# Expert stage of a four-layer megakernel: fourth buffers for split weights and rows, and the weight split moved ahead of the gate

## The chip, the cores and the metric

The kernel runs on one core of a Trainium2 chip. A core has five engines that run their own instruction streams in order and meet only at semaphores: TensorE (PE in the rows, its weight loads PEld), VectorE (DVE), ScalarE (ACT), GpSimd (POOL) and SyncE (SP), which here only starts DMA transfers. The metric is the device time of one execution in microseconds (us).

## The reference, cut to what matters

The program is a stack of four layers on x of 8 x 128 tokens by 256 features. Each layer is a normalised cross attention and then a feed-forward part with a mixture of experts. The change touches only the routed experts of the second layer:

```python
T = 1024 tokens, K = 4, E = 32 experts, C = 2*T*K//E = 256 rows each, H = 256, I = 128
buf = zeros((E, C, H)).at[sorted_eid, pos].set(x[tok], mode='drop')   # rows gathered by expert
gu = einsum('ech,ehf->ecf', buf, w13);  g, u = split(gu, 2, axis=-1)
act = silu(g) * u
eo = einsum('eci,eih->ech', act, w2)
out_slots = eo[sorted_eid, pos]                                       # and back to the tokens
```

## The kernel before, in words

Everything is written by hand: each engine's stream is a Python function, all orders are those of the code, and semaphores carry the dependencies. Before the expert stage the normalised rows of all tokens are scattered in DRAM to the `seats` of their experts. Then 32 experts pass through one software pipeline, one expert per turn of the loop.

For expert k the work is this. SP loads 384 KB of float32 weights (`expert_weights`, L549) and 288 KB of rows (`expert_rows`, L556: 256 rows of 256 features and 32 numbers of destination). PE turns the rows with four float32 transposes (`expert_turn`, L1520). ACT and DVE split the turned rows in a high and a low float16 part (`expert_x`: ACT L1062 twice, DVE L2451 twice, then DVE L2454 for the destinations). The weights are split in the same way (`expert_split`: ACT L1054 high, then DVE L2460 low). PE does gate and up with 12 matmuls (L1535). ACT takes silu of the gate (L1070), DVE multiplies it by up (`expert_gated`, L2470), ACT and DVE split the product (`expert_h`: L1078, L2476), PE does the down product with 6 matmuls (L1550), ACT copies it out (`expert_out`, L1086), and POOL scatters it in two indirect transfers (L749) to `slots` in DRAM.

The orders of one turn k of the loop are:
- PE: turn k+1, gate and up k, down k-1.
- ACT: rows' high part k+1, silu k, weights' high part k+2, product's high part k, copy out k-1.
- DVE: rows' low parts and destinations k+1, product k, weights' low part k+2, product's low part k.
- SP: weights k+3, rows k+2, and the last output row of expert k-2 (L562), which waits until expert k-2 has been copied out (`e_y`). So each transfer behind it starts only after that copy.

There are four buffers of raw weights (`e_w`), but three of split weights (`e_split`) and three of rows (`e_x`). The split of expert k+2 therefore waits for the down product of expert k-1 (`e_down`), and the rows of k+2 wait until those of k-1 are turned and their destinations read. After the last expert SP waits for all scatters and loads the `slots` back.

Of the kernel before, what the change touches and what calls it, by code (L numbers as in the profile page):

```python
# [26 lines left out]
F16 = mybir.dt.float16  # L27
# [4 lines left out]
ACT = mybir.ActivationFunctionType  # L32
AX = mybir.AxisListType

P = 128
B, S, D = 8, 128, 256
# [9 lines left out]
E0, F0, FS0 = 8, 176, 352  # L46
SHARED0 = -(-FS0 // P)
E1, F1 = 32, 128
# [29 lines left out]
def build(nc, a, out):  # L78

    with ExitStack() as ctx:  # L80
# [23 lines left out]
        ident = sb("ident", [P, P])  # L104
# [51 lines left out]
        class Arena:  # L156
# [4 lines left out]
            def take(self, shape, dt=F32, rows=P):  # L161
# [27 lines left out]
        ar = Arena()  # L189
# [21 lines left out]
        ar = Arena()  # L211
        f_s = ar.take([2, HALF])
        f_g = ar.take([2, HALF])
        f_h = ar.take([2, HALF])
# [4 lines left out]
        f_wT = ar.take([T], rows=E0)  # L219
        f_cmp = ar.take([B, E0, E0])  # L220
        f_eq = ar.take([B, E0, E0])
        f_rk = ar.take([B, E0])
# [18 lines left out]
        m_place = ar.take([B, E1])  # L241
        m_w = ar.take([B, TOP1])
        m_dest = ar.take([E1, CT]).bitcast(U32)
        e_x = ar.take([3, CT, ROW])
        wq_f = arena[:, ar.at:ar.at + T].rearrange("p (w o d) -> p w o d", w=2, o=KD)
        wq_diag = arena[:, ar.at:ar.at + HALF].rearrange("p (k o) -> p k o", k=4)
        e_xT = ar.take([2, 2, KD, CAPACITY], F16)
# [6 lines left out]
        last_rows = k3_raw[0:E1, :]  # L254
        e_w = [W[:, 1, :], wb[:, :, :].rearrange("p a b -> p (a b)")[:, 0:WROW],
               wb[:, :, :].rearrange("p a b -> p (a b)")[:, WROW:2 * WROW], W[:, 0, :]]
        e_split = [W16[:, 1, :, :], e_w16, W16[:, 0, :, :]]
        x_rms = xn


# [175 lines left out]
        def _(sp):  # L436
# [114 lines left out]
            def expert_rows(k):  # L551

                if k >= 3:
                    sp.wait_ge(sem("e_turn"), k - 2)
                    sp.wait_ge(sem("e_dest"), k - 2)
                sp.dma_start(e_x[:, k % 3, :, :], seats[k * CAPACITY:(k + 1) * CAPACITY, :].rearrange("(p c) d -> p c d", c=CT))\  # L556
                    .then_inc(sem("ex_in", k % 3), 16)

            def last_row(k):

# [11 lines left out]
            def loads_1():  # L572
                for k in range(4):
                    expert_weights(k)
                sp.wait_ge(sem("seated"), 16 * B * TOP1)
                for k in range(3):
                    expert_rows(k)
                for k in range(E1):
                    if k >= 1 and k + 3 < E1:
                        expert_weights(k + 3)  # L580
                    if k >= 1 and k + 2 < E1:
                        expert_rows(k + 2)
                    if k >= 2:
# [246 lines left out]
        def _(act):  # L830
# [216 lines left out]
            def expert_split(k):  # L1047

                act.wait_ge(sem("slot_in", k % 4), 16 * (k // 4 + 1))
                if k == 2:  # L1050
                    act.wait_ge(sem("down_done"), tiles(2))
                if k >= 3:
                    act.wait_ge(sem("e_down"), k - 2)
                nc.scalar.activation(e_split[k % 3][:, 0, :], e_w[k % 4], ACT.Copy, scale=WSCALE).then_inc(sem("ew_hi"), 1)  # L1054

            def expert_x(k):

# [288 lines left out]
        def _(pe):  # L1346
# [163 lines left out]

            def expert_turn(k):

                pe.wait_ge(sem("ex_in", k % 3), 16 * (k // 3 + 1))
                if k < 2:
                    pe.wait_ge(sem("gated"), EXPERT)
                else:
                    pe.wait_ge(sem("e_xlo"), KD * (k - 1))
                for c in range(KD):
                    for r in range(CT):
                        last = nc.tensor.transpose(ps[:, k % 2, c * CAPACITY + r * P:c * CAPACITY + (r + 1) * P],  # L1520
                                                   e_x[:, k % 3, r, c * P:(c + 1) * P], ident[:, :])
                last.then_inc(sem("e_turn"), 1)

            def expert_gate_up(k):

                pe.wait_ge(sem("ew_lo"), k + 1)
                pe.wait_ge(sem("e_xlo"), KD * (k + 1))
                if k >= 2:
                    pe.wait_ge(sem("gated"), EXPERT + k - 1)
                else:  # L1530
                    pe.wait_ge(sem("wi"), 2)
                for g in range(2):
                    for c in range(KD):
                        for i, w in THREE:
                            last = nc.tensor.matmul(ps[:, 2 + k % 2, g * CAPACITY:(g + 1) * CAPACITY],  # L1535
                                                    e_split[k % 3][:, w, g * D + c * P:g * D + (c + 1) * P],
                                                    e_xT[:, k % 2, i, c, :], start=(g == 0 and c == 0 and i + w == 0),
                                                    stop=(c == KD - 1 and w == 1), skip_group_check=True)
                last.then_inc(sem("gu_done"), 1)

            def expert_down(k):

                pe.wait_ge(sem("h_lo"), EXPERT + k + 1)
                if k < 2:
                    pe.wait_ge(sem("shared_read"), 1)
                else:
                    pe.wait_ge(sem("e_y"), k - 1)
                for r in range(CT):
                    for w, i in THREE:
                        last = nc.tensor.matmul(ps[:, 4 + k % 2, r * D:(r + 1) * D], f_h16[:, k % 2, i, r * P:(r + 1) * P],  # L1550
                                                e_split[k % 3][:, w, 2 * D:3 * D], start=(r == 0 and i + w == 0),
                                                stop=(w == 1), skip_group_check=True)
                last.then_inc(sem("e_down"), 1)

# [446 lines left out]
        def _(dve):  # L2001
# [445 lines left out]
            def expert_x(k):  # L2447

                dve.wait_ge(sem("e_xhi"), KD * (k + 1))
                for c in range(KD):  # L2450
                    nc.vector.scalar_tensor_tensor(e_xT[:, k % 2, 1, c, :], ps[:, k % 2, c * CAPACITY:(c + 1) * CAPACITY],  # L2451
                                                   normw[:, c:c + 1], e_xT[:, k % 2, 0, c, :], ALU.mult, ALU.subtract)\
                        .then_inc(sem("e_xlo"), 1)
                nc.vector.tensor_scalar(m_dest[:, k, :], e_x[:, k % 3, :, D + k], -1.0, NOWHERE, ALU.mult, ALU.add)\  # L2454
                    .then_inc(sem("e_dest"), 1)

            def expert_split(k):

                dve.wait_ge(sem("ew_hi"), k + 1)
                nc.vector.scalar_tensor_tensor(e_split[k % 3][:, 1, :], e_w[k % 4], WSCALE, e_split[k % 3][:, 0, :],  # L2460
                                               ALU.mult, ALU.subtract).then_inc(sem("ew_lo"), 1)

            def expert_gated(k):
# [488 lines left out]
```

## Time and profile before

| | us |
|---|---|
| median of 3 runs | 1033.53 (1028.81 to 1034.68) |
| the profiled execution, its own time | 1037.46 |
| its span, first to last instruction | 1035.6 |
| busy in the span: PE / DVE / ACT / POOL | 859.2 / 677.9 / 521.2 / 326.0 |

The expert stage runs from about 304 to 426 us of the span. A row of a timeline names the start, the duration, the engine, the line, the operation with output and input, and in brackets how long the engine had been idle and what released it. `arena`, `W` and `wb` are on-chip memory that several names share (`e_x`, `f_h16`, `e_y` and one split buffer lie in `arena`), `ps` is PSUM, `in_w` the weights in DRAM.

### The profile page before, as it was taken

To read this page: it belongs to the slowest core of one execution; us is meant where nothing else is said; L and a number is where in the kernel's file an instruction comes from. 1 tells how busy PE (TensorE), PEld (TensorE's weight loads), DVE (VectorE), ACT (ScalarE), POOL (GpSimd) and SP (SyncE) were. 2 spreads that over 40 slices of the span, in tenths; PEclk is the share of its full clock that TensorE was granted. 3 is DMA by queue.
4 is the path that set the end of the run, shared out by engine and by line. 5 is a ranking of instruction groups with operands and counts; after the bars stand their busy time and mean duration, and the time that the engine had idled before them with its cause. 6 is when DMAs were issued, how large, how long until landed. Compare 5 with 4: busy or idle time off the path is not lost. (4 is left out here: it accounts for less than half of the span.)

```text
span 1035.6 us, 17165 instructions
## 1 busy us (share of the span) xinstructions
PE 859.2 (83%) x6369; PEld 532.9 (51%) x6369; DVE 677.9 (65%) x1402; ACT 521.2 (50%) x840; POOL 326.0 (31%) x267
## 2 busy tenths in 40 slices
PE   5978999776227776797979998778799999999997
PEld 3434665463216564574545554445455556555554
DVE  7985888787817667266336479645778657744343
ACT  4714345445117767336558743455456786533332
POOL 2531343312744555303025662100355333200000
PEclk9988999988659999897879999999999999999999
DMA  8973433310246677331013453111256445433332
GB/s 267 324 254 107 129 107 114 93 33 1 114 151 189 211 225 218 117 113 46 18 32 122 123 170 106 46 32 47 70 174 182 129 129 167 144 105 95 107 94 85
DMA packets 60191, 129.12 MB, mean 125 GB/s; under 512 B 9267, under 2 KB 25025, under 8 KB 60114
## 3 DMA queue, kind: packets, MB, share of 16 engines
q1 hardware_dynamic: 55506, 119.17, 37.4%
q0 software_dynamic: 4608, 8.94, 2.3%
q8 instruction: 47, 0.77, 0.3%
q14 instruction: 30, 0.25, 0.1%
HBM read 83.95 MB, written 48.27 MB: 128 GB/s over the span
## 5 line engine op out<-in xcount | busy, mean ns | idle before, releaser
L1448 PE MATMUL ps<-turned_buf,W 128*128 128x512 f16 x576 | 136.8, 388 | 5.7 <-DVE ctx_sb L2280 1.8
L2280 DVE SCALAR_TENSOR_TENSOR ctx_sb<-ps,ctx_sb 128x512 f32<-128x512 f32 x96 | 66.2, 690 | 111.0 <-PE ps L1448 80.7
L1448 PE MATMUL ps<-turned_buf,wb 128*128 128x512 f16 x576 | 133.5, 382 | 0.0
L2287 DVE TENSOR_TENSOR ctxT<-ctx_sb,ctxT 128x512 f16<-128x512 f32 x96 | 71.4, 744 | 70.7 <-ACT ctxT L1023 70.2
L761 POOL TENSOR_SCALAR W<-W 128x768 f32<-128x768 f32 x32 | 68.6, 2145 | 127.8 <-ACT wb L1035 64.1
L1023 ACT ACTIVATE ctxT<-ctx_sb 128x512 f16<-128x512 f32 x96 | 60.2, 627 | 94.4 <-DVE ctx_sb L2280 94.3
L1015 ACT ACTIVATE ctx_sb<-ps 128x512 f32<-128x512 f32 x96 | 57.3, 597 | 99.3 <-PE ps L1448 99.0
L1448 PEld LDWEIGHTS ps<-turned_buf,W 128*128 128x128 f16 x576 | 56.1, 100 | 69.1 <-issue 8.0
L1391 PE MATMUL ps<-turned_buf,W 128*128 128x512 f16 x360 | 87.3, 396 | 2.5 <-issue 2.5
L1448 PEld LDWEIGHTS ps<-turned_buf,wb 128*128 128x128 f16 x576 | 56.1, 99 | 59.8 <-issue 2.7
L749 POOL DMA_INDIRECT slots<-arena x64 | 62.3, 973 | 68.6 <-ACT arena L1086 56.3
L1464 PE MATMUL ps<-W,ctxT 128*128 128x256 f16 x576 | 70.8, 273 | 5.4 <-DVE x L2296 3.7
L1464 PE MATMUL ps<-wb,ctxT 128*128 128x256 f16 x576 | 72.0, 276 | 3.8 <-DVE ctxT L2287 3.2
L705 POOL TENSOR_TENSOR arena<-arena,wb 128x512 f32<-128x512 f32 x28 | 42.6, 1523 | 87.9 <-DVE arena L2221 87.9
L1464 PEld LDWEIGHTS ps<-wb,ctxT 128*128 128x128 f16 x576 | 55.6, 99 | 21.5 <-DVE ctxT L2287 4.9
L1464 PEld LDWEIGHTS ps<-W,ctxT 128*128 128x128 f16 x576 | 54.4, 98 | 23.2 <-issue 10.9
L1391 PEld LDWEIGHTS ps<-turned_buf,W 128*128 128x128 f16 x360 | 36.2, 101 | 43.4 <-issue 9.6
L1520 PE MATMUL ps<-ident,arena 128*128 128x128 f32 x128 | 22.5, 305 | 41.0 <-DMA arena<-seats 36.8
L678 POOL TENSOR_TENSOR rstd<-veps,mhalf 128x4 f32<-128x4 f32 x13 | 14.5, 1118 | 129.8 <-DVE veps L2019 129.8
L2296 DVE SCALAR_TENSOR_TENSOR x<-ps,arena,x 128x256 f32<-128x256 f32 x128 | 52.9, 475 | 2.4 <-PE ps L1464 2.4
L1403 PE MATMUL ps<-W,arena 128*128 128x256 f16 x360 | 45.5, 279 | 9.6 <-DVE arena L2228 9.6
L988 ACT ACTIVATE arena<-arena 128x512 f16<-128x512 f32 x30 | 18.7, 629 | 56.7 <-POOL arena L705 56.5
(411 smaller groups left out, 1719.4 us busy)
## 6 DMA issues: line engine op xcount, KB each, us to landing
W<-in_w SPq DMA_DIRECT2D x77, 384.0 KB, 3.6
seats<-k_st SPq DMA_DIRECT2D x8, 1152.0 KB, 10.9
arena<-seats SPq DMA_DIRECT2D x32, 288.0 KB
kept<-W SPq DMA_DIRECT2D x24, 384.0 KB, 4.0
kept<-wb SPq DMA_DIRECT2D x24, 384.0 KB, 4.2
W<-kept SPq DMA_DIRECT2D x24, 384.0 KB
wb<-kept SPq DMA_DIRECT2D x24, 384.0 KB
wb<-in_w SPq DMA_DIRECT2D x18, 384.0 KB, 11.2
```

The lines of the kernel that those rows point to most:

```text
L705: nc.gpsimd.tensor_tensor(f_h[:, half, :], f_g[:, half, :], wb[:, k % 2, half * HALF:(half + 1) * HALF], ALU.mult).then_inc(sem("h_full"), 1)
L749: nc.gpsimd.indirect_dma_start(slots, bass.IndirectOffsetOnAxis(ap=m_dest[:, k, c:c + 1], axis=0), e_y[k % 3][:, c, :], None, bounds_check ...
L761: link(nc.gpsimd.tensor_scalar(W[:, n % 2, :], W[:, n % 2, :], WSCALE, None, ALU.mult))
L1015: nc.scalar.activation(h_s[:, g % 2, :], bank(4), ACT.Silu, scale=1.0 / WSCALE).then_inc(sem("silu_done"), 1)
L1023: nc.scalar.activation(h_16[:, g % 2, 0, :], h_g[:, g % 2, :], ACT.Copy).then_inc(sem("h_hi"), 1)
L1391: last = nc.tensor.matmul(bank(2 * g + half), W16[:, k % 2, w, g * D + c * P:g * D + (c + 1) * P], x16[:, i, c, half * HALF:(half + 1) * H ...
L1403: last = nc.tensor.matmul(ps[:, 4 + t // 2, (t % 2) * D:(t % 2 + 1) * D], f_h16[:, k % 2, i, t * S:(t + 1) * S], W16[:, k % 2, w, 2 * D:3 ...
L1448: last = nc.tensor.matmul(bank(4 + n), w4[k % 4][:, w, n * D + c * P:n * D + (c + 1) * P], x16[:, i, c, half * HALF:(half + 1) * HALF], st ...
L1464: last = nc.tensor.matmul(ps[:, 6 + t // 2, (t % 2) * D:(t % 2 + 1) * D], h_16[:, g % 2, i, t * S:(t + 1) * S], w4[k % 4][:, w, 2 * D:3 * ...
L2280: nc.vector.scalar_tensor_tensor(h_g[:, g % 2, :], bank(5), 1.0 / WSCALE, h_s[:, g % 2, :], ALU.mult, ALU.mult).then_inc(sem("gated"), 1)
L2287: nc.vector.tensor_tensor(h_16[:, g % 2, 1, :], h_g[:, g % 2, :], h_16[:, g % 2, 0, :], ALU.subtract)\
L2296: ins = nc.vector.scalar_tensor_tensor(x[:, t, :], ps[:, 6 + t % 4 // 2, (t % 2) * D:(t % 2 + 1) * D], l_w[:, L - 2, t, e:e + 1], x[:, t, ...
```

## The change

Split weights and rows get a fourth buffer each. The fourth split buffer lies where `f_h` of the first layer was, the fourth buffer of rows where the first layer's router compared its scores. On ACT and on DVE the split of expert k+2 moves ahead of the silu and the product of expert k. SP issues the rows one expert further ahead (k+3 in place of k+2) and ahead of the weights.

```diff
-        e_x = ar.take([3, CT, ROW])
+        e_rows = ar.take([3, CT, ROW])
+        e_x = [e_rows[:, k, :, :] for k in range(3)] + \
+            [arena[:, f_cmp_at:f_cmp_at + CT * ROW].rearrange("p (c d) -> p c d", c=CT)]
...
-        e_split = [W16[:, 1, :, :], e_w16, W16[:, 0, :, :]]
+        e_split = [W16[:, 1, :, :], e_w16, arena[:, f_h_at:f_h_at + WROW].bitcast(F16).rearrange("p (i d) -> p i d", i=2),
+                   W16[:, 0, :, :]]
...
             def expert_rows(k):
-                if k >= 3:
-                    sp.wait_ge(sem("e_turn"), k - 2)
-                    sp.wait_ge(sem("e_dest"), k - 2)
+                if k >= 4:
+                    sp.wait_ge(sem("e_turn"), k - 3)
+                    sp.wait_ge(sem("e_dest"), k - 3)
...
-                for k in range(3):
+                for k in range(4):
                     expert_rows(k)
                 for k in range(E1):
                     if k >= 1 and k + 3 < E1:
+                        expert_rows(k + 3)
                         expert_weights(k + 3)
-                    if k >= 1 and k + 2 < E1:
-                        expert_rows(k + 2)
...
             def expert_split(k):          # ACT
                 act.wait_ge(sem("slot_in", k % 4), 16 * (k // 4 + 1))
-                if k == 2:
+                if k == 3:
                     act.wait_ge(sem("down_done"), tiles(2))
-                if k >= 3:
-                    act.wait_ge(sem("e_down"), k - 2)
+                if k >= 4:
+                    act.wait_ge(sem("e_down"), k - 3)
...
                 for k in range(E1):       # ACT
                     if k + 1 < E1:
                         expert_x(k + 1)
-                    expert_silu(k)
                     if k + 2 < E1:
                         expert_split(k + 2)
+                    expert_silu(k)
                     expert_h(k)
...
             for k in range(E1):           # DVE
                 if k + 1 < E1:
                     expert_x(k + 1)
-                expert_gated(k)
                 if k + 2 < E1:
                     expert_split(k + 2)
+                expert_gated(k)
                 expert_h(k)
```

The order of instructions on ACT in a turn in the middle of the stage, before. L1062 is the rows' high part, L1070 silu, L1054 the weights' high part, L1078 the product's high part, L1086 the copy out:

```order
L1062 ACTIVATE arena<-ps,normw 128x256 x2
L1070 ACTIVATE arena<-ps 128x256
L1054 ACTIVATE arena<-W 128x768
L1078 ACTIVATE arena<-arena 128x256
L1086 ACTIVATE arena<-ps 128x512
```

And in the changed kernel, where the same lines stand five lines later (L1067, L1059, L1075, L1083, L1091):

```order
L1067 ACTIVATE arena<-ps,normw 128x256 x2
L1059 ACTIVATE arena<-wb 128x768
L1075 ACTIVATE arena<-ps 128x256
L1083 ACTIVATE arena<-arena 128x256
L1091 ACTIVATE arena<-ps 128x512
```

The weights' part has moved from between silu and the product's part to ahead of silu.

The order on DVE in the same place, before. L2451 is the rows' low part, L2454 the destinations, L2470 the product of silu and up, L2460 the weights' low part, L2476 the product's low part:

```order
L2451 SCALAR_TENSOR_TENSOR arena<-ps,normw,arena 128x256 x2
L2454 TENSOR_SCALAR arena<-arena 128x2
L2470 SCALAR_TENSOR_TENSOR arena<-ps,arena 128x256
L2460 SCALAR_TENSOR_TENSOR arena<-W,arena 128x768
L2476 TENSOR_TENSOR arena<-arena 128x256
```

And in the changed kernel (L2456, L2459, L2465, L2475, L2481):

```order
L2456 SCALAR_TENSOR_TENSOR arena<-ps,normw,arena 128x256 x2
L2459 TENSOR_SCALAR arena<-arena 128x2
L2465 SCALAR_TENSOR_TENSOR W<-W 128x768
L2475 SCALAR_TENSOR_TENSOR arena<-ps,arena 128x256
L2481 TENSOR_TENSOR arena<-arena 128x256
```

The product, for which ACT's L1083 waits, now stands behind the weights' low part.

## Rows read from the trace of the kernel before

**Rows 1.** The expert stage: length, busy us of PE, PEld, DVE, ACT, POOL, granted clock, DMA share, GB/s

```profile
304.00:420.00 116.00, 88.58 (x675) 67.65 (x676) 79.13 (x183) 82.31 (x184) 54.50 (x56) 0.94 0.66 205
```

**Rows 2.** The transposes of rows (L1520): count, then what ended the idle time before

```profile
L1520 PE MATMUL ps<-ident,arena x128: 272/273/476, 303.9 to 417.8; 128*128 128x128 f32 x128
...
  DMA arena<-seats: 80.3, 32
```

**Rows 3.** Timeline of ACT, one undisturbed turn of the loop

```profile
313.12 0.84 ACT L1054 ACTIVATE W<-W 128x768 f16<-128x768 f32 x1 [0.64 <-PE ps L1550]
313.88 0.40 ACT L1078 ACTIVATE arena<-arena 128x256 f16<-128x256 f32 x1
314.18 0.58 ACT L1086 ACTIVATE arena<-ps 128x512 f32<-128x512 f32 x1
314.66 0.83 ACT L1062 ACTIVATE arena<-ps,normw 128x256 f16<-128x256 f32 x2
315.37 0.39 ACT L1070 ACTIVATE arena<-ps 128x256 f32<-128x256 f32 x1
316.27 0.84 ACT L1054 ACTIVATE arena<-W 128x768 f16<-128x768 f32 x1 [0.51 <-PE ps L1550]
317.02 0.40 ACT L1078 ACTIVATE arena<-arena 128x256 f16<-128x256 f32 x1
```

**Rows 4.** Timeline of DVE in the same turn

```profile
314.00 0.96 DVE L2460 SCALAR_TENSOR_TENSOR W<-W 128x768 f16<-128x768 f32 x1 [0.67 <-ACT W L1054]
314.88 0.42 DVE L2476 TENSOR_TENSOR arena<-arena 128x256 f16<-128x256 f32 x1
315.52 0.88 DVE L2451 SCALAR_TENSOR_TENSOR arena<-ps,normw,arena 128x256 f16<-128x256 f32 x2 [0.23 <-ACT arena L1062]
316.31 0.25 DVE L2454 TENSOR_SCALAR arena<-arena 128x2 uint32<-128x2 f32 x1
316.38 0.42 DVE L2470 SCALAR_TENSOR_TENSOR arena<-ps,arena 128x256 f32<-128x256 f32 x1
```

**Rows 5.** Timeline of PE in the same turns and the next

```profile
312.20 0.83 PE L1550 MATMUL ps<-W,arena 128*128 128x256 f16 x6
...
315.35 0.83 PE L1550 MATMUL ps<-arena 128*128 128x256 f16 x6 [0.57 <-DVE arena L2476]
...
318.50 0.83 PE L1550 MATMUL ps<-W,arena 128*128 128x256 f16 x6 [0.53 <-issue]
319.54 0.66 PE L1520 MATMUL ps<-ident,arena 128*128 128x128 f32 x4 [0.21 <-DMA arena<-seats]
```

**Rows 6.** Timeline of ACT, the end of the stage

```profile
418.77 0.58 ACT L1086 ACTIVATE arena<-ps 128x512 f32<-128x512 f32 x1
...
423.47 0.42 ACT L1078 ACTIVATE arena<-arena 128x256 f16<-128x256 f32 x1 [0.49 <-DVE arena L2470]
...
425.38 0.60 ACT L1086 ACTIVATE arena<-ps 128x512 f32<-128x512 f32 x1 [0.86 <-PE ps L1550]
```

**Rows 7.** Timeline of DVE, the product before that

```profile
423.01 0.42 DVE L2470 SCALAR_TENSOR_TENSOR arena<-ps,arena 128x256 f32<-128x256 f32 x1 [0.72 <-issue]
```

**Rows 8.** Timeline of SP's queue, two issues of rows

```profile
316.09 0.38 SPq L556 DMA_DIRECT2D arena<-seats  x1
...
340.04 0.38 SPq L556 DMA_DIRECT2D arena<-seats  x1
```

**Rows 9.** Timeline of PE, the transposes that used the second of them

```profile
345.99 0.66 PE L1520 MATMUL ps<-ident,arena 128*128 128x128 f32 x4 [0.94 <-DMA arena<-seats]
```

**Rows 10.** Timeline of ACT, two later turns

```profile
320.34 0.84 ACT L1054 ACTIVATE W<-wb 128x768 f16<-128x768 f32 x1 [1.31 <-PE ps L1550]
...
368.77 0.38 ACT L1070 ACTIVATE arena<-ps 128x256 f32<-128x256 f32 x1 [2.35 <-remote]
```

**Rows 11.** What SP's queue waited for in the stage: us, times, longest

```profile
SPq L562 <- ACT arena L1086: 64.7, 29, 6.5
```

**Rows 12.** Timeline of POOL, the last scatter

```profile
429.54 0.97 POOL L749 DMA_INDIRECT slots<-arena  x1 [0.30 <-issue]
```

More of the change, by code:

```diff
@@ L213, in build @@
         f_g = ar.take([2, HALF])
+        f_h_at = ar.at
         f_h = ar.take([2, HALF])
@@ L219, in build @@
         f_wT = ar.take([T], rows=E0)
+        f_cmp_at = ar.at
         f_cmp = ar.take([B, E0, E0])
@@ L243, in build @@
         m_dest = ar.take([E1, CT]).bitcast(U32)
-        e_x = ar.take([3, CT, ROW])
+        e_rows = ar.take([3, CT, ROW])
+        assert CT * ROW <= 2 * B * E0 * E0
+        e_x = [e_rows[:, k, :, :] for k in range(3)] + \
+            [arena[:, f_cmp_at:f_cmp_at + CT * ROW].rearrange("p (c d) -> p c d", c=CT)]
         wq_f = arena[:, ar.at:ar.at + T].rearrange("p (w o d) -> p w o d", w=2, o=KD)
@@ L551, in expert_rows @@
             def expert_rows(k):
-                if k >= 3:
-                    sp.wait_ge(sem("e_turn"), k - 2)
-                    sp.wait_ge(sem("e_dest"), k - 2)
-                sp.dma_start(e_x[:, k % 3, :, :], seats[k * CAPACITY:(k + 1) * CAPACITY, :].rearrange("(p c) d -> p c d", c=CT))\
-                    .then_inc(sem("ex_in", k % 3), 16)
+                if k >= 4:
+                    sp.wait_ge(sem("e_turn"), k - 3)
+                    sp.wait_ge(sem("e_dest"), k - 3)
+                sp.dma_start(e_x[k % 4], seats[k * CAPACITY:(k + 1) * CAPACITY, :].rearrange("(p c) d -> p c d", c=CT))\
+                    .then_inc(sem("ex_in", k % 4), 16)
             def last_row(k):
@@ L1049, in expert_split @@
                 act.wait_ge(sem("slot_in", k % 4), 16 * (k // 4 + 1))
-                if k == 2:
+                if k == 3:
                     act.wait_ge(sem("down_done"), tiles(2))
-                if k >= 3:
-                    act.wait_ge(sem("e_down"), k - 2)
-                nc.scalar.activation(e_split[k % 3][:, 0, :], e_w[k % 4], ACT.Copy, scale=WSCALE).then_inc(sem("ew_hi"), 1)
+                if k >= 4:
+                    act.wait_ge(sem("e_down"), k - 3)
+                nc.scalar.activation(e_split[k % 4][:, 0, :], e_w[k % 4], ACT.Copy, scale=WSCALE).then_inc(sem("ew_hi"), 1)
             def expert_x(k):
@@ L1511, in expert_turn @@
             def expert_turn(k):
-                pe.wait_ge(sem("ex_in", k % 3), 16 * (k // 3 + 1))
+                pe.wait_ge(sem("ex_in", k % 4), 16 * (k // 4 + 1))
                 if k < 2:
@@ L1520, in expert_turn @@
                         last = nc.tensor.transpose(ps[:, k % 2, c * CAPACITY + r * P:c * CAPACITY + (r + 1) * P],
-                                                   e_x[:, k % 3, r, c * P:(c + 1) * P], ident[:, :])
+                                                   e_x[k % 4][:, r, c * P:(c + 1) * P], ident[:, :])
                 last.then_inc(sem("e_turn"), 1)
@@ L1535, in expert_gate_up @@
                             last = nc.tensor.matmul(ps[:, 2 + k % 2, g * CAPACITY:(g + 1) * CAPACITY],
-                                                    e_split[k % 3][:, w, g * D + c * P:g * D + (c + 1) * P],
+                                                    e_split[k % 4][:, w, g * D + c * P:g * D + (c + 1) * P],
                                                     e_xT[:, k % 2, i, c, :], start=(g == 0 and c == 0 and i + w == 0),
@@ L1550, in expert_down @@
                         last = nc.tensor.matmul(ps[:, 4 + k % 2, r * D:(r + 1) * D], f_h16[:, k % 2, i, r * P:(r + 1) * P],
-                                                e_split[k % 3][:, w, 2 * D:3 * D], start=(r == 0 and i + w == 0),
+                                                e_split[k % 4][:, w, 2 * D:3 * D], start=(r == 0 and i + w == 0),
                                                 stop=(w == 1), skip_group_check=True)
@@ L2453, in expert_x @@
                         .then_inc(sem("e_xlo"), 1)
-                nc.vector.tensor_scalar(m_dest[:, k, :], e_x[:, k % 3, :, D + k], -1.0, NOWHERE, ALU.mult, ALU.add)\
+                nc.vector.tensor_scalar(m_dest[:, k, :], e_x[k % 4][:, :, D + k], -1.0, NOWHERE, ALU.mult, ALU.add)\
                     .then_inc(sem("e_dest"), 1)
@@ L2459, in expert_split @@
                 dve.wait_ge(sem("ew_hi"), k + 1)
-                nc.vector.scalar_tensor_tensor(e_split[k % 3][:, 1, :], e_w[k % 4], WSCALE, e_split[k % 3][:, 0, :],
+                nc.vector.scalar_tensor_tensor(e_split[k % 4][:, 1, :], e_w[k % 4], WSCALE, e_split[k % 4][:, 0, :],
                                                ALU.mult, ALU.subtract).then_inc(sem("ew_lo"), 1)
```

## The prediction

> **What bounds the kernel now.** The page comes first, for the engines' totals, then the windows of the expert stage, then the groups of waits inside it, then the timelines of ACT, DVE and PE over two turns of the loop that nothing disturbs, and last the queue of SP. The stage takes 116 us in which PE is busy 88.58, ACT 82.31 and DVE 79.13 [rows 1]. No engine is full, so a chain across engines sets the pace. Outside the stage the change moves nothing.
>
> The copy-out of expert 0 starts at 314.18 [rows 3], that of expert 28 at 418.77, with three more behind it, the last at 425.38 [rows 6]. That is 28 turns in 104.6 us, 3.74 us each.
>
> An undisturbed turn is shorter. The down product of one expert starts at 312.20 and the next at 315.35, the one after at 318.50 [rows 5]: 3.15 us, twice. The rows close the loop. The down product takes 0.83, ends at 313.03, and releases ACT's split of the weights at 313.12 [rows 3], because its buffer is the one which that product read. DVE's low part starts at 314.00, the product's low part behind it at 314.88 and takes 0.42 [rows 4], and the next down product starts at 315.35 [rows 5]. So 0.83 + 0.09 + 0.88 + 0.88 + 0.42 + 0.05 = 3.15. Three buffers of split weights make this loop.
>
> At that pace 28 turns would take 88.2 us. The other 16.4 us are lost in single turns. The waits of PE's transposes name the loads of rows every time [rows 2] (27.4 us of that total are the wait for the first rows, before the stage). Rows issued at 316.09 [rows 8] were used at 319.54 [rows 5], 3.45 us later; those issued at 340.04 [rows 8] only at 345.99 [rows 9], 5.95 us later. SP issues them late since its queue stands behind the last row of an older expert: 64.7 us of waiting for ACT's copy-out [rows 11]. A late transpose costs more than its own wait: the down product before it should have ended at 318.50 + 0.83 = 319.33, but ACT's split, which it releases, starts at 320.34 [rows 5, 10]. Once silu starts 2.35 us late though its input had been computed long before by the rows of PE [rows 10]; I count this with the 16.4 us.
>
> **The change part by part.**
>
> The fourth buffer of split weights. The split of k+2 now waits for the down product of k-2 in place of k-1. That product is a whole turn older, so the loop of 3.15 us is cut. By itself this is a gain, down to what the next chain allows.
>
> The fourth buffer of rows, and their place in SP's queue. Rows k+3 are issued where rows k+2 were. They have one turn more, at least 3.15 us, in front of the slowest transfer seen, 5.95 us. I expect the transposes' waits to go inside the stage, and with them most of the 16.4 us. The weights are issued one rows' issue later (0.38 us [rows 8]) and are split somewhat earlier in the turn. Their lead is about two turns and a half, over 8 us, so the shift is hidden. If that cover is gone it comes back as a wait of ACT, which is the third rival below.
>
> The new order. It adds no instruction, it moves two. Before, ACT's split of the weights filled the time in which DVE made the product of silu and up; the product stood ahead of the weights' low part on DVE. Now DVE does the rows' low parts and the destinations, waits for ACT's high part of the weights, does their low part, and only then the product. ACT's next instruction after silu, the product's high part, waits for all of it, and behind that instruction stand the copy-out and the rows of the next expert. So ACT and DVE go round together:
> - ACT rows' high part to DVE's rows' low part: 315.52 - 314.66 = 0.86 [rows 3, 4]
> - low parts and destinations, to DVE's next instruction: 316.38 - 315.52 = 0.86 [rows 4]
> - weights' low part, to DVE's next: 314.88 - 314.00 = 0.88 [rows 4]
> - the product: 0.42 [rows 4]
> - to ACT's waiting high part: 423.47 - (423.01 + 0.42) = 0.04 [rows 6, 7]
> - high part to copy-out: 314.18 - 313.88 = 0.30 [rows 3]
> - copy-out to the rows' high part of the next expert: 314.66 - 314.18 = 0.48 [rows 3]
>
> The sum is 3.84 us a turn. No buffer is in this loop, so no buffer can shorten it. Is PE able to follow? It was busy 88.58 us in about 31 turns, 2.85 us each, and now none of its results is needed at once: silu comes behind the split, and a product ends more than a turn before it is copied out. PE therefore runs ahead and waits. A delay of one to two us on PE is taken up by that lead, which is why I set the remaining stalls to nothing. Bounds for the turn: the same ring entered through ACT's split (0.71 from the rows to ACT's next instruction, 0.88 to DVE's low part, then 0.88 + 0.42 + 0.04 + 0.30 + 0.48 [rows 3, 4, 6, 7]) gives 3.71. That would hold if DVE's rows were never late. Above, the 16.4 us may stay in part. I take 3.84, since both of its first terms stand in every undisturbed turn.
>
> The first turns: the split of expert 2 moves into idle time, the copy-out of expert 0 gets the new order once; I put it at +0.3 us (0 to +1). In the last turns there is no split and the order is the old one. The last scatter starts at 429.54 [rows 12], behind POOL's own queue, and only shifts with the rest.
>
> **The sum.** 28 x 3.84 = 107.5 us in place of 104.6, and 0.3 at the start: +3.2 us. The profiled execution took 1037.46 us, of which 1.9 lie around its span of 1035.6. The changed kernel would take 1037.46 + 3.2 = 1040.7. The median of the runs before is 1033.5, 3.9 lower. If those runs differ outside this stage, the new median is 1036.8. If they lost 3.9 us less to late rows, which the new order swallows anyway, it is 1040.7. I take the middle, 1039.
>
> By the Trainium skill (Perfetto Trace Analysis, section Optimization Strategy) the same gap repeating on an engine can mean too little SBUF for the next tile, so too few buffers. ACT's repeated 0.51 us before the split is such a gap [rows 3], and two buffers are added here. That rule leads to the first rival.
>
> **The rivals.**
>
> Faster: the buffers decide, not the order. If the product did not have to wait for the weights' low part, for instance because the split runs so far ahead that it is over when silu ends, the turn would be 3.15 us or below, down to PE's 2.85. That gives 88.2 - 104.6 = -16.4 us, or -24.8. For it: the stalls on rows are real and the change goes for them. Against it: ACT's split comes directly behind the rows' high part of the same turn, so DVE cannot have its low part done before 0.86 + 0.86 + 0.88 us into the turn. It decides if DVE's product follows ACT's silu within 0.1 us. Time: 1033.5 - 16.4 + up to 3.9, about 1019.
>
> Slower still: the stalls stay on top of the 3.84 us. For it: one late silu had no late transfer that I can name. Against: PE's lead. With half of 16.4 left it is 1047, with all 1055.
>
> The clock: PE's granted clock is 0.94 in the stage [rows 1], nearly always the upper of its two levels (2.4 GHz). If the regular pauses of PE put it on 1.2 GHz, a turn would be 2 x 2.85 = 5.7 us, 28 of them 160 us, the whole 1088. Against: PE's share, 2.85 of 3.84, is 0.74 where it was 0.76.
>
> **How the numbers follow.** The forecast, a ring of 3.7 to 3.9 us with little left of the stalls, has 0.72, its own range is 1035 to 1044. The faster rival has 0.13, stalls on top 0.13, the clock 0.02. About 0.5%, 5.2 us, is what a measurement of this kernel tells from no change. The border at 1038.7 cuts the forecast: 0.40 of its 0.72 lie above, 0.31 within, 0.01 below. So slower is 0.40 + 0.13 + 0.02 = 0.55, same 0.31, faster 0.01 + 0.13 = 0.14. The range 1033 to 1046 leaves out the faster rival, the clock and the worse third of the stalls, 0.2 in all.
>
> **What would show it.** In the changed profile the copy-outs should follow each other every 3.8 to 3.9 us with little scatter. The wait of PE's transposes for rows should be the first one alone. ACT should wait before the product's high part in every turn, about 1 us, for DVE's product, and DVE's product should start when the weights' low part lets it, over 0.5 us after silu's end. PE should wait for DVE before gate and up or down. I am wrong if the turns are 3.2 us or shorter, or if ACT waits for transfers of weights, or if the stage keeps turns of 5 us.

## The result, and the profile after

Seven runs of each kernel on one chip: 1032.53 us median before (1028.69 to 1036.47), 1042.71 us changed (1038.09 to 1046.10). The difference of the medians is 10.2 us, the ratio 1.0107 with a 95% interval of 1.0073 to 1.0141: the changed kernel is slower. The profiled execution of the changed kernel took 1046.10 us, its span is 1044.2.

The stage in the same window as [rows 1]:

```profile
304.00:420.00 116.00, 84.32 (x666) 63.95 (x666) 77.60 (x183) 78.32 (x179) 63.82 (x56) 0.98 0.62 199
```

PE and ACT are less busy than before in the same 116 us (84.32 in place of 88.58, 78.32 in place of 82.31): fewer turns fit into them. The granted clock is 0.98 where it was 0.94; both windows hold the stage's first turns, before which PE had stood still, and from 312 on the changed kernel has 1.00.

The transposes of rows, as in [rows 2]; the second row is the idle time in front of them by releaser, with the number of waits:

```profile
L1525 PE MATMUL ps<-ident,arena x128: 272/273/477, 301.7 to 417.4; 128*128 128x128 f32 x128
...
  DMA arena<-seats: 54.9, 2
```

Two waits in place of 32, both of them the first wait before the stage (about 27.4 us, counted once for PE and once for its weight load). No transpose inside the stage waits for its rows any more. This row counts PE and PEld together. Before, the 32 were 13 waits of PE (36.8 us) and 19 of PEld (43.4 us), so PE itself waited 12 times and 9.4 us inside the stage.

One turn on ACT, to be read against [rows 3]. L1067 is the rows' high part, L1059 the weights' high part, L1075 silu, L1083 the product's high part, L1091 the copy-out:

```profile
323.50 0.58 ACT L1091 ACTIVATE arena<-ps 128x512 f32<-128x512 f32 x1
323.97 0.83 ACT L1067 ACTIVATE arena<-ps,normw 128x256 f16<-128x256 f32 x2
324.68 0.85 ACT L1059 ACTIVATE W<-W 128x768 f16<-128x768 f32 x1
325.42 0.39 ACT L1075 ACTIVATE arena<-ps 128x256 f32<-128x256 f32 x1
327.01 0.42 ACT L1083 ACTIVATE arena<-arena 128x256 f16<-128x256 f32 x1 [1.21 <-DVE arena L2475]
327.34 0.58 ACT L1091 ACTIVATE arena<-ps 128x512 f32<-128x512 f32 x1
327.81 0.83 ACT L1067 ACTIVATE arena<-ps,normw 128x256 f16<-128x256 f32 x2
```

The same turn on DVE, against [rows 4]. L2456 is the rows' low part, L2459 the destinations, L2465 the weights' low part, L2475 the product, L2481 the product's low part:

```profile
324.84 0.88 DVE L2456 SCALAR_TENSOR_TENSOR arena<-ps,normw,arena 128x256 f16<-128x256 f32 x2 [0.79 <-ACT arena L1067]
325.63 0.25 DVE L2459 TENSOR_SCALAR arena<-arena 128x2 uint32<-128x2 f32 x1
325.69 0.95 DVE L2465 SCALAR_TENSOR_TENSOR W<-W 128x768 f16<-128x768 f32 x1
326.56 0.42 DVE L2475 SCALAR_TENSOR_TENSOR arena<-ps,arena 128x256 f32<-128x256 f32 x1
327.46 0.42 DVE L2481 TENSOR_TENSOR arena<-arena 128x256 f16<-128x256 f32 x1 [0.48 <-ACT arena L1083]
```

These twelve rows hold the result. ACT's rows at 323.97, DVE's rows at 324.84, weights' low part at 325.69, product at 326.56, ending at 326.98, ACT's product high part at 327.01, copy-out at 327.34, next rows at 327.81. From 323.97 to 327.81 are 3.84 us. ACT stands still for 1.21 us in front of L1083; silu was over at 325.81, but DVE's product started only 0.75 us later, behind the weights.

PE in the same time, against [rows 5]. L1555 is down, L1525 the transposes, L1540 gate and up:

```profile
324.11 0.83 PE L1555 MATMUL ps<-W,arena 128*128 128x256 f16 x6 [0.66 <-DVE arena L2481]
324.77 0.60 PE L1525 MATMUL ps<-ident,arena 128*128 128x128 f32 x4
325.81 1.48 PE L1540 MATMUL ps<-arena 128*128 128x256 f16 x12 [0.44 <-issue]
327.94 0.83 PE L1555 MATMUL ps<-arena 128*128 128x256 f16 x6 [0.66 <-DVE arena L2481]
```

The down products start at 324.11 and 327.94, 3.83 us apart, and PE has pauses of 0.4 and 0.7 us in each turn. All waits of ACT for DVE's product in the stage:

```profile
ACT arena L1083 <- DVE arena L2475: 37.1, 32, 1.2
```

32 waits, 37.1 us. The copy-outs of experts 0, 28 and 31, as in [rows 3, 6]:

```profile
311.97 0.58 ACT L1091 ACTIVATE arena<-ps 128x512 f32<-128x512 f32 x1
```

```profile
419.60 0.58 ACT L1091 ACTIVATE arena<-ps 128x512 f32<-128x512 f32 x1
...
426.10 0.60 ACT L1091 ACTIVATE arena<-ps 128x512 f32<-128x512 f32 x1 [0.89 <-PE ps L1555]
```

From 311.97 to 419.60 are 107.6 us for 28 turns, which the prediction put at 107.5. Every one of these turns takes 3.84 to 3.89 us. ACT never waits for a transfer of weights in the stage. SP's queue still waits for ACT's copy-out (72.5 us where it was 64.7), so it is the lead of one turn more that hides the rows' transfers, not an earlier end of that wait.

### The profile page after: what moved, and what is told of

Its sections match the earlier page's. It is cut to its first block and busy times, and to the rows that moved or that the text cites. A ratio compares the mean times of both kernels' runs of the same rounds, so it can differ in the third digit from the quotient of the medians.

```text
span 1044.2 us, 17163 instructions
## 1 busy us (share of the span) xinstructions
PE 862.5 (83%) x6369; PEld 532.3 (51%) x6369; DVE 677.2 (65%) x1402; ACT 519.1 (50%) x840; POOL 335.1 (32%) x267
## 5 line engine op out<-in xcount | busy, mean ns | idle before, releaser
L1020 ACT ACTIVATE ctx_sb<-ps 128x512 f32<-128x512 f32 x96 | 57.2, 596 | 100.6 <-PE ps L1453 100.4
L754 POOL DMA_INDIRECT slots<-arena x64 | 71.6, 1119 | 62.3 <-ACT arena L1091 51.5
L1469 PE MATMUL ps<-W,ctxT 128*128 128x256 f16 x576 | 73.0, 278 | 5.4 <-DVE x L2301 3.7
L2456 DVE SCALAR_TENSOR_TENSOR arena<-ps,normw,arena 128x256 f16<-128x256 f32 x64 | 28.0, 480 | 46.1 <-ACT arena L1067 46.1
```

The lines of the kernel that those rows point to most:

```text
L754: nc.gpsimd.indirect_dma_start(slots, bass.IndirectOffsetOnAxis(ap=m_dest[:, k, c:c + 1], axis=0), e_y[k % 3][:, c, :], None, bounds_check ...
L1020: nc.scalar.activation(h_s[:, g % 2, :], bank(4), ACT.Silu, scale=1.0 / WSCALE).then_inc(sem("silu_done"), 1)
L1469: last = nc.tensor.matmul(ps[:, 6 + t // 2, (t % 2) * D:(t % 2 + 1) * D], h_16[:, g % 2, i, t * S:(t + 1) * S], w4[k % 4][:, w, 2 * D:3 * ...
```

## The experiments

All times of 28 turns are those from the copy-out of expert 0 to that of expert 28. Ratios are to the kernel before, timed beside it on the same chip, with a 95% interval. The experiments ran on different chips, so times of two kernels are compared directly only where both stood beside the kernel before on one of them.

| kernel | 28 turns, us | undisturbed turn | ratio of the time to before |
|---|---|---|---|
| before, four profiles | 104.6, 100.4, 96.3, 95.5 | 3.15 | |
| changed, two profiles | 107.6, 107.7 | 3.84 | 1.0107 [1.0073, 1.0141], 1.0139 [1.0097, 1.0182] |
| order only | 114.3 | 4.06 | 1.0086 [1.0048, 1.0124] |
| changed, DVE's order undone | 95.7 | 3.13 | 0.9853 [0.9793, 0.9913] |
| changed, both orders undone, two profiles | 90.8, 83.7 | 2.97 | 0.9851 [0.9796, 0.9906], 0.9873 [0.9811, 0.9934] |
| changed, copy-out ahead | 93.4 | 3.36 | 0.9982 [0.9942, 1.0023] |
| rows only | 88.5 | 3.15 | 0.9901 [0.9874, 0.9928] |
| split buffers only | 92.9 | 2.97 | 0.9963 [0.9931, 0.9995] |
| both orders undone, copy-out ahead | 74.2 | mostly 2.5 to 2.67 (mean of all: 2.65) | 0.9831 [0.9790, 0.9872] |

### The order undone on both engines

```diff
                     if k + 1 < E1:            # ACT
                         expert_x(k + 1)
+                    expert_silu(k)
                     if k + 2 < E1:
                         expert_split(k + 2)
-                    expert_silu(k)
                     expert_h(k)
...
+                expert_gated(k)               # DVE
                 if k + 2 < E1:
                     expert_split(k + 2)
-                expert_gated(k)
```

> The changed kernel with its order on ACT and DVE undone: silu and product stand ahead of the split again; four buffers of split weights, four of rows, rows ahead of weights on SP's queue stay. Theory (the ring through DVE's weights' low part holds every turn at 3.84 us): the ring is gone and the loop over three split buffers too, so a turn is about 3.0 us (ACT's own instructions), without stalls on rows; 28 turns 84 us in place of 107.6, the time 20 to 24 us below the changed kernel and 10 to 17 us below the kernel before. Rival (the buffers, their places in memory or the earlier loads of rows cost the time): turns stay near 3.8 us or scattered, and the time is within 4 us of the changed kernel.

Measured: 1027.15 us median against 1039.66 for the kernel before on that chip, 12.5 us less as expected, ratio 0.9851. The undisturbed turn is 2.97 us. The 28 turns took 90.8 us, not 84: single turns had 0.3 to 1.5 us more, though hardly any transpose waited for rows. So it was run again:

> The changed kernel with the order undone on both engines, once more. Its first profile had 7.6 us over 28 turns of 2.97 us without any wait for rows, which the run with only rows changed (0.3 us over 3.15) and the run with the copy-out ahead did not have. If those were chance of that run or chip: 83 to 85 us for 28 turns now. If they belong to the kernel: 88 us or more again. Time in the first case 14 to 18 us below before.

Measured: 83.7 us for 28 turns, one of them 3.26 and the others 2.97 to 3.02; 1017.73 us against 1029.92, ratio 0.9873. The expected time was 14 to 18 us below before, the measured one is 12. The 7 us over do not come in every run of this kernel. Whether they go with the chip or with the run is not shown, since the second run was on another chip. One turn of the second run, on ACT (same names as above):

```profile
333.18 0.42 ACT L1083 ACTIVATE arena<-arena 128x256 f16<-128x256 f32 x1 [0.34 <-DVE arena L2475]
333.50 0.58 ACT L1091 ACTIVATE arena<-ps 128x512 f32<-128x512 f32 x1
333.98 0.83 ACT L1067 ACTIVATE arena<-ps,normw 128x256 f16<-128x256 f32 x2
334.69 0.39 ACT L1075 ACTIVATE arena<-ps 128x256 f32<-128x256 f32 x1
334.96 0.86 ACT L1059 ACTIVATE W<-W 128x768 f16<-128x768 f32 x1
```

From the product's high part at 333.18, copy-out, rows at 333.98, silu 334.69, split 334.96. The turn before had its copy-out at 330.53, this one at 333.50: 2.97 us, which is 3.84 less the 0.88 of DVE's weights. The ring is still there, without that one term. I had expected ACT's own instructions to set the turn; but ACT waits 0.34 us for DVE's product, so a ring of both engines still does.

### The order undone on DVE alone

```diff
             for k in range(E1):               # DVE
                 if k + 1 < E1:
                     expert_x(k + 1)
+                expert_gated(k)
                 if k + 2 < E1:
                     expert_split(k + 2)
-                expert_gated(k)
```

> The changed kernel with the order undone on DVE alone: ACT still does the split ahead of silu, DVE does the product ahead of the weights' low part. Theory: ACT's wait before the product's high part shrinks from 1.2 to about 0.5 us, the ring becomes ACT's rows, split, silu, product, high part, copy-out: about 3.15 us a turn, time 17 to 20 us below the changed kernel. Rival (it is the split's place on ACT that costs): the turn stays at 3.7 us or more.

Measured: 1026.06 us against 1039.66, ratio 0.9853; undisturbed turns of 3.13 us. The split still stands ahead of silu on ACT:

```profile
328.44 0.58 ACT L1091 ACTIVATE arena<-ps 128x512 f32<-128x512 f32 x1
328.92 0.83 ACT L1067 ACTIVATE arena<-ps,normw 128x256 f16<-128x256 f32 x2
329.64 0.85 ACT L1059 ACTIVATE arena<-wb 128x768 f16<-128x768 f32 x1
330.37 0.39 ACT L1075 ACTIVATE arena<-ps 128x256 f32<-128x256 f32 x1
331.25 0.42 ACT L1083 ACTIVATE arena<-arena 128x256 f16<-128x256 f32 x1 [0.49 <-issue]
```

ACT's wait before L1083 is 0.49 us, as expected, where the changed kernel has 1.21. So most of the cost is one line on one engine: the weights' low part ahead of the product on DVE, 0.71 of the 0.87 us between 3.84 and 2.97. The split's place on ACT costs the other 0.16. The 28 turns took 95.7 us, 8.0 over 28 x 3.13, though no transpose in the stage waited for rows. The time expected against the changed kernel can't be checked, for no time of that kernel on this chip is on record; against before it is 13.6 us less.

### The order alone

```diff
-                    expert_silu(k)            # in the kernel before, ACT
                     if k + 2 < E1:
                         expert_split(k + 2)
+                    expert_silu(k)
...
-                expert_gated(k)               # and DVE
                 if k + 2 < E1:
                     expert_split(k + 2)
+                expert_gated(k)
```

> The kernel before with only the new order on ACT and DVE; three buffers of each and the old queue of SP. Theory: the ring holds as in the changed kernel, and now the split also waits for a down product that comes late, so a turn is 3.85 to 4.0 us; with late rows on top at most a few us; time 3 to 8 us above the changed kernel, 12 to 18 above before. Rival (without the buffers the order costs nothing): the time of the kernel before within 4 us.

Measured: 1050.01 us against 1039.66, +10.4 in the medians; the ratio, 1.0086, says a little less. Turns of 4.06 us, a little over the 3.85 to 4.0 expected, all but one of them (4.65) within 0.02. The 10.4 us above before are fewer than the 12 to 18 expected. Two copy-outs on ACT (L1086) and what stands between (L1062 rows, L1054 split, L1078 product's high part):

```profile
331.38 0.58 ACT L1086 ACTIVATE arena<-ps 128x512 f32<-128x512 f32 x1
331.86 0.83 ACT L1062 ACTIVATE arena<-ps,normw 128x256 f16<-128x256 f32 x2
332.92 0.84 ACT L1054 ACTIVATE W<-W 128x768 f16<-128x768 f32 x1 [0.23 <-PE ps L1550]
...
335.12 0.42 ACT L1078 ACTIVATE arena<-arena 128x256 f16<-128x256 f32 x1 [1.09 <-DVE arena L2470]
335.44 0.58 ACT L1086 ACTIVATE arena<-ps 128x512 f32<-128x512 f32 x1
```

Rows to split take 1.06 us here (331.86 to 332.92), since the split has to wait for the down product which reads its buffer; in the changed kernel it is 0.71. That is the ring entered through ACT's split, which the prediction had as its lower bound of 3.71: with 1.06 in place of 0.71 it sums to 4.06, now longer than 3.84, and so it sets the turn. The buffers together are worth about 0.2 us a turn under the new order. I had expected the time 3 to 8 us above the changed kernel; the two were not timed on one chip, so only the turns can be compared: 114.3 against 107.6 us.

### Rows alone

```diff
-        e_x = ar.take([3, CT, ROW])           # in the kernel before
+        e_rows = ar.take([3, CT, ROW])
+        e_x = [e_rows[:, k, :, :] for k in range(3)] + \
+            [arena[:, f_cmp_at:f_cmp_at + CT * ROW].rearrange("p (c d) -> p c d", c=CT)]
...
                     if k >= 1 and k + 3 < E1:
+                        expert_rows(k + 3)
                         expert_weights(k + 3)
-                    if k >= 1 and k + 2 < E1:
-                        expert_rows(k + 2)
```

> The kernel before with only the fourth buffer of rows and the new place of rows in SP's queue; three split buffers, old order. Theory of the prediction (late rows make the excess over 3.15 us, 16.4 and 12.2 us in two profiles): turns 3.15 us with nearly nothing on top, 28 turns 88 to 91 us, time 10 to 15 us below before. Rival (PE's results come late by themselves, as they did in the run with the old order, where 7.6 us were left): turns 3.15 us with 7 to 9 us on top, 28 turns 95 to 98 us, time 4 to 8 us below before.

Measured: 1020.52 us against 1029.74, 9.2 us less where 10 to 15 were expected, ratio 0.9901. 28 turns take 88.5 us, that is 28 x 3.15 and 0.3 more. The fourth buffer and the new place in SP's queue were not tried apart. The transposes' waits (L1524 in this kernel), and the stage in a window:

```profile
L1524 PE MATMUL ps<-ident,arena x128: 272/273/473, 302.6 to 400.3; 128*128 128x128 f32 x128
...
  DMA arena<-seats: 55.3, 3
```

```profile
312.00:407.00 95.00, 77.84 (x655) 61.12 (x653) 75.82 (x177) 78.42 (x179) 57.37 (x60) 1.00 0.75 230
```

Three waits in place of 32, all before the stage's steady part, and a granted clock of 1.00. So the waits for rows, and the lateness that came with them, went. One part of the excess is not settled by this run: silus that start late though their input was ready. The first profile of before has four of them in the stage, released by `remote`, which means that the profile knows no instruction to put the release down to (us, times, longest):

```profile
ACT arena L1070 <- remote: 7.4, 4, 2.4
```

The second has two (2.5 us). The third and the fourth, on another chip, have none, and neither has the run with split buffers only, which was on the chip of this one and kept its waits for rows. The first runs with both orders undone and with DVE's undone have them (3.1 and 4.3 us) without waits for rows. So their absence here may belong to the chip. If nothing changed outside the stage, the 9.2 us saved in the medians are about what the median run of before lost to late rows on this chip.

### The fourth split buffer alone

```diff
-        e_split = [W16[:, 1, :, :], e_w16, W16[:, 0, :, :]]
+        e_split = [W16[:, 1, :, :], e_w16, arena[:, f_h_at:f_h_at + WROW].bitcast(F16).rearrange("p (i d) -> p i d", i=2),
+                   W16[:, 0, :, :]]
...
-                if k >= 3:
-                    act.wait_ge(sem("e_down"), k - 2)
+                if k >= 4:
+                    act.wait_ge(sem("e_down"), k - 3)
```

> The kernel before with only the fourth buffer of split weights, old order, three buffers of rows. Theory: undisturbed turns of 2.97 us in place of 3.15 (5 us over 28), the waits for rows stay, 28 turns 96 to 101 us, time 2 to 6 us below before. Rival (the loop over three split buffers does not bound): turns stay at 3.15.

Measured: 1024.21 us against 1029.74, ratio 0.9963. The undisturbed turn is 2.97 us, so the loop over three split buffers did bound at 3.15. The waits for rows stay:

```profile
PE ps L1522 <- DMA arena<-seats: 18.7, 20, 1.8
```

20 waits of PE with 18.7 us, and 28 turns of 92.9 us, under the 96 to 101 I had expected: 9.7 us over 28 x 2.97. The time is 5.5 us below before in the medians, within the 2 to 6 expected.

### The copy-out ahead, with the new order

```diff
+                    if k:                     # in the changed kernel, ACT
+                        expert_out(k - 1)
                     expert_h(k)
-                    if k:
-                        expert_out(k - 1)
```

> The changed kernel with one edit: on ACT the copy-out of expert k-1 stands ahead of the high part of product k. The split stays ahead of silu and product on both engines. Theory (the ring's sum): the copy-out's 0.48 us leaves the ring of 3.84, so every turn is 3.36 us and 28 turns take 94.1 us, 13.5 below the changed kernel. Rival (some engine's load or a buffer holds 3.84): no change, or the turns scatter.

Measured: every turn from the second on is 3.35 to 3.38 us, 28 turns 93.4 us (the first took 2.76). 1028.66 us against 1029.92, ratio 0.9982: no difference from the kernel before that can be told.

```profile
330.96 0.42 ACT L1083 ACTIVATE arena<-arena 128x256 f16<-128x256 f32 x1 [0.72 <-DVE arena L2475]
331.29 0.82 ACT L1067 ACTIVATE arena<-ps,normw 128x256 f16<-128x256 f32 x2
...
333.00 0.61 ACT L1091 ACTIVATE arena<-ps 128x512 f32<-128x512 f32 x1
334.32 0.42 ACT L1083 ACTIVATE arena<-arena 128x256 f16<-128x256 f32 x1 [0.72 <-DVE arena L2475]
334.64 0.82 ACT L1067 ACTIVATE arena<-ps,normw 128x256 f16<-128x256 f32 x2
```

L1091, the copy-out, now fills ACT's wait for the product, which is down from 1.21 to 0.72 us, and L1083 follows L1083 after 3.36 us (330.96, 334.32). A sum of rows predicted this to 0.01 us. So it is this ring that holds the changed kernel: taking one of its terms out shortened the turn by that term.

### The copy-out ahead, with the old order

The two diffs of the first and the last experiment together: old order on ACT and DVE, copy-out ahead of the product's high part.

> The changed kernel with its order undone on ACT and DVE, and on ACT the copy-out of expert k-1 put ahead of the high part of product k, so that it fills the time in which DVE makes the product. Theory (the remaining ring of 2.97 us is ACT rows, DVE rows, product, high part, copy-out): the copy-out's 0.48 us leaves the ring, and the turn falls to what PE and ACT are busy, 2.7 to 2.9 us; 28 turns 3 to 7 us below the 90.8 us of the run with the old order; time 2 to 7 us below that kernel, 14 to 20 below before. Rival (PE or POOL bounds already, or late results eat it): no gain within 2 us.

Measured: 1011.64 us against 1029.74, ratio 0.9831, 18 us below before; 28 turns in 74.2 us. This is faster than I expected (3 to 7 us below 90.8; it is 16.6 below, or 9.5 below the second profile of the old order, 83.7). It has the lowest ratio of all here, though the interval overlaps those of the kernels with DVE's or both orders undone; in the stage it is the shortest by far. The ring of 2.97 less 0.48 would be 2.49 us; the shortest turns take 2.49 to 2.50, most others up to 2.67.

```profile
330.97 0.42 ACT L1083 ACTIVATE arena<-arena 128x256 f16<-128x256 f32 x1
331.27 0.84 ACT L1067 ACTIVATE arena<-ps,normw 128x256 f16<-128x256 f32 x2
332.00 0.39 ACT L1075 ACTIVATE arena<-ps 128x256 f32<-128x256 f32 x1
332.28 0.84 ACT L1059 ACTIVATE W<-W 128x768 f16<-128x768 f32 x1
333.01 0.59 ACT L1091 ACTIVATE arena<-ps 128x512 f32<-128x512 f32 x1
333.49 0.42 ACT L1083 ACTIVATE arena<-arena 128x256 f16<-128x256 f32 x1
```

```profile
312.00:393.00 81.00, 77.17 (x662) 62.50 (x661) 73.84 (x179) 77.34 (x178) 58.88 (x61) 1.00 0.82 271
```

In these rows ACT goes from one instruction into the next, with no wait in brackets: 77.34 us busy of 81. PE is busy 77.17. DVE is busy 73.84. With ACT and PE at 95% of the window and DVE at 91%, little is left to fill; which of them bounds the stage at 2.65 us a turn was not tried.

### The kernel before and the changed one, again

> The kernel before once more, for a second profile. If the turns' excess over 3.15 us varies by chance, the 28 turns sum to something other than 104.6 us: between 96 and 106 us. If it is fixed by the program, 104.6 within 0.5 us.

> The kernel before, a third profile. Theory (the stalls on rows vary from run to run and are what the before runs differ by): 28 turns in 90 to 106 us, undisturbed turns 3.15 us. Rival (fixed): 100 to 105.

> The kernel before, a fourth profile, to the same question as the third: whether 104.6 us for 28 turns was high among its runs. If the ratio of the timed runs (1.0107, 1.0139) comes from the stage, some profiles must show 92 to 98 us.

Measured: 100.4, 96.3 and 95.5 us for 28 turns, at times of the same profiled executions of 1032.85, 1033.18 and 1033.25 us. The undisturbed turn is 3.15 in each. The 104.6 us on which the prediction's sum stood was the highest of four. The second ran on one chip and the last two on another, so the spread may hold differences of chips as well as of runs; the last two differ by 0.8 us. How a single turn is lost, in the fourth profile, on PE and on ACT:

```profile
328.25 0.82 PE L1550 MATMUL ps<-W,arena 128*128 128x256 f16 x6
332.07 0.66 PE L1520 MATMUL ps<-ident,arena 128*128 128x128 f32 x4 [3.01 <-DMA arena<-seats]
```

```profile
332.76 0.84 ACT L1062 ACTIVATE arena<-ps,normw 128x256 f16<-128x256 f32 x2 [1.97 <-PE ps L1520]
```

The transposes wait 3.01 us for rows, ACT's next work waits 1.97 us for the transposes, and the turn takes 5.64 us.

> The changed kernel once more, beside the kernel before on one chip, with a second profile. Theory (the ring, and no stalls): 28 turns in 107.6 us within 0.5 us again; the ratio to before lies between 1.003 and 1.012, and what exceeds the 3 to 7 us of the stage goes with PE's mean granted clock of the runs, outside the stage. Rival (the change costs something outside the stage): in runs of the same mean clock the changed kernel is more than 9 us slower than before.

Measured: 1043.92 us against 1029.74, ratio 1.0139. The second profile has 107.7 us for 28 turns. The ratio lies above the 1.003 to 1.012 that I expected. And the mark which I had set for the rival was passed: at a mean granted clock of 0.935 to 0.939 the changed kernel took 1039.33 and 1039.79 us, before 1023.22, 1025.78, 1027.02 and 1028.92, so 10 to 17 us less. But the mark was set wrong, for it supposed that before never has less than 98 us in the stage, and two of its profiles have 95.5 and 96.3. What is outside the stage can be compared directly: up to the first copy-out, the last three turns, and from the last copy-out to the end, the changed kernel has 312.6 + 6.5 + 610.7 = 929.8 us, the second profile of before 312.8 + 7.2 + 610.6 = 930.6. Over all profiles the time outside the 28 turns is 929.8 and 936.6 us in the changed kernel, and 930.6 to 936.0 in the four of before. A cost outside the stage, if there is one, is lost in that spread. Before was not profiled on the chip of this comparison.

## Why the prediction was right, and where its size was off

The mechanism came out as told, step by step. The transposes' waits in the stage went. ACT and DVE go round together at 3.84 us a turn (predicted 3.84). 28 turns take 107.6 us (predicted 107.5). ACT waits 1.21 us before each product's high part (predicted about 1). PE has pauses and follows. PE's clock stayed up, so that rival is out. The remaining stalls on top, the slower rival, did not come: no turn takes more than 3.89, in two profiles. The 0.3 us at the start did not show: the first copy-out came at 311.97 and 312.61 us, before at 312.76 to 314.18.

Some smaller readings were wrong, and did not carry the result. The waits of 80.3 us [rows 2] hold the first wait twice, so about 55 us of them lie before the stage and not 27.4; and they are not every wait of the transposes, which had 8.0 us more of idle time under `issue`. Silu came late four times, not once. The 2.85 us of PE a turn is no floor: it counts the first turns at the lower clock (0.57 from 304 to 312 us), and the last experiment has turns of 2.65. And the list of rivals has none for lost cover of the weights, to which the part on SP's queue points; no such wait came.

The first rival, that the buffers decide and not the order, fell with the order undone on DVE alone (3.13 us a turn) and with the copy-out ahead (3.36). It had a true half, though. Without the new order the two buffers and SP's new order save 12 to 13 us of the whole, the low end of what it said (12.5 to 16.4). The Trainium skill's rule (Perfetto Trace Analysis, section Optimization Strategy), that a repeated gap can mean too few buffers, is borne out for ACT's gap by the run with one more split buffer: 3.15 to 2.97 us a turn. But the changed kernel, with both fourth buffers, shows a repeated gap of 1.21 us on ACT that comes from the order in which the two engines take turns.

The term that was mis-sized is the stage before, "in place of 104.6". The prediction allowed for it by halves: the middle between 1036.8 and 1040.7, which came to 1039 where 1042.7 was measured, +5.5 us where it was +10.2 (ratio 1.0107), inside the range of 1033 to 1046. Four profiles now give 95.5 to 104.6 us for the same program, 99.2 in the mean, so the change costs 3.0 to 12.2 us in the stage, 8.4 in the mean. The run with rows alone says the same from the other side: it took 9.2 us off the median, so the median run of before on its chip loses about that much, not 16.4. 28 x 3.84 less (28 x 3.15 + 9.2) is 10.1 us, and 10.2 was measured. That this fits to 0.1 us is luck: on the chip of the run with rows alone the changed kernel was 14.2 us slower than before (ratio interval 1.0097 to 1.0182, 10.0 to 18.7 us). The better base for the sum was what the timed runs have, not the one profile, and the 3.9 us by which the profile lay above their median was the hint that it was high. I gave it half its weight, and that the forecast still fell inside the range owes something to the range's width.

The late silus, which I counted with the late rows, may be a thing of their own. The first runs with both orders undone and with DVE's undone, on one chip, had late turns without waits for rows, 7.6 and 8.0 us in sum, with such silus among them; on two other chips no profile has such a silu. What makes them is open; it was not tried. In the changed kernel they cost nothing that shows: ACT waits for DVE in every turn, as the prediction said of PE's lead.

## What to carry to other kernels

Before adding buffers, write down the ring that two in-order engines make when each waits once a turn for the other, and add its terms from the start times of one undisturbed turn; the turn cannot be shorter than that sum, and here it was exact to 0.01 us in three kernels. Do not put a long instruction that nobody waits for yet (0.88 us of splitting) ahead of a short one that the other engine waits for; put something that is ready into the wait, as the copy-out here, worth 0.5 us a turn under the new order and 0.3 under the old. And when single turns are lost to late transfers, one profile is one draw: a stage's time should be taken from several, or from what its undisturbed turns say plus a spread.

## What the runs showed of the hardware that I had not expected

PE's results can be seen by ACT later than PE's rows say. In [rows 5] the transposes wait 0.21 us for rows, yet the down product before them, which should have ended at 319.33 by its row, releases ACT only at 320.34 [rows 10]. The Trainium skill (Perfetto Trace Analysis, section Tensor Engine Instruction (MATMUL, LD_WEIGHTS)) says that the profiler computes the end of a matmul and does not observe it, which leaves room for a result later than its row, though no run here shows by how much. PE's own wait for rows may be what holds the result back: with rows in time the whole excess fell to 0.3 us over 28 turns. But it can't be all of it. In the first run with both orders undone one silu starts only at 400.62, while its gate and up had ended at 398.43 by their row, and no transpose after 306 us waited for rows:

```profile
400.62 0.38 ACT L1075 ACTIVATE arena<-ps 128x256 f32<-128x256 f32 x1 [1.69 <-remote]
```

The cause was not tried by itself, and stays open.

The rest of the program, which no kernel here changed, took 609.5 to 620.8 us from the last copy-out to the end, and mostly went with the mean granted clock of the execution: 610.7 at 0.935 and 618.1 at 0.931 in the two profiles of the changed kernel, 620.8 at 0.924 in the first with both orders undone; the first profile of before is an exception with 610.2 at 0.930. 23 runs of the kernel before on one chip lay between 1023.2 us at a clock of 0.939 and 1035.3, which occurs at 0.925 and at 0.932. A difference of a few us between two medians of this program can go with the clock outside the stage; the stage's own time is the sharper measure.
